# A sample-conditional adapter and linear layer on one core: half of the up projection in rounded parts, and x turned one sample ahead

## The reference

```python
h = relu(x @ W1[lang] + b1[lang])          # 512 -> 128: the up projection
y = x + h @ W2[lang] + b2[lang]            # 128 -> 512: the down projection
n = (y - mean(y)) * rsqrt(var(y) + 1e-5)   # over the 512 channels
x1 = x + n * gamma[lang] + beta[lang]
out = x1 + x1 @ W[cat] + b[cat]            # 512 -> 512
```

## Time and profile before

| what | value |
|---|---|
| median of 3 runs | 632.99 us (631.51 to 633.32) |
| the profiled execution | 632.66 us |
| its span in the trace | 630.8 us |
| instructions | 11158 |
| TensorE matmul (PE) busy | 620.4 us, 98% |
| VectorE (DVE) busy | 524.0 us, 83% |
| ScalarE (ACT) busy | 466.2 us, 74% |
| GpSimd (POOL) busy | 413.6 us, 66% |
| chain that ended last, share by engine | PE 95%, DVE 2%, DMA 1%, issue 1% |
| DMA | 166.00 MB, mean 263 GB/s |

### The profile page before, as it was taken

One profiled execution on the slowest core, in us unless ns is written; L12 is line 12 of the kernel. 1 busy time (PEld: TensorE's weight loads), 2 busy tenths in 40 slices (PEclk: granted clock), 3 DMA queues, 4 the chain that ended last, 5 costly groups with the idle time before them and its releaser, 6 DMA issues.

```text
span 630.8 us, 11158 instructions
## 1 busy us (share of the span) xinstructions
PE 620.4 (98%) x2773; PEld 474.5 (75%) x2773; DVE 524.0 (83%) x1155; ACT 466.2 (74%) x709; POOL 413.6 (66%) x326
## 2 busy tenths in 40 slices
PE   8799999999999999999999999999999999999997
PEld 7567877777877777877777877777877777877786
DVE  1879888889888889888889888889888889888873
ACT  3777777787777887777787777787777787777770
POOL 3947766666766666767666866766866766866630
PEclk9899999999999999999999999999999999999999
DMA  8848899888899888899898899988899798899422
GB/s 303 265 143 247 285 295 297 262 255 276 280 294 300 258 255 275 289 287 308 259 252 274 280 291 292 274 263 259 288 286 312 253 257 274 279 289 316 167 85 100
DMA packets 125562, 166.00 MB, mean 263 GB/s; under 512 B 10834, under 2 KB 72284, under 8 KB 121456
## 3 DMA queue, kind: packets, MB, share of 16 engines
q1 hardware_dynamic: 93540, 149.59, 72.6%
q10 hardware_dynamic: 32012, 16.30, 10.7%
HBM read 132.17 MB, written 33.55 MB: 263 GB/s over the span
## 4 chain that ended last, share of the span: by engine, by line
PE 95%; DVE 2%; DMA 1%; issue 1%; ACT 0%; ACTq 0%; SPq 0%; DVEq 0%
PE o_bank L730 18%; PE o_bank L728 18%; PE o_bank L729 18%; PE d_bank L756 17%; PE n_bank L744 9%; PE y_bank L728 2%; PE d_bank L728 2%; PE y_bank L730 2%; PE d_bank L730 2%; PE y_bank L729 2%; PE d_bank L729 2%; DMA x_tok<-in_x 1%; DVE y L587 0%; DVE xT L693 0%; PE n_bank L806 0%
## 5 line engine op out<-in xcount | busy, mean ns | idle before, releaser
L364 POOL TENSOR_TENSOR w_lo<-w_raw,w_hi 128x512 fp32r<-128x512 f32 x128 | 163.1, 1296 | 160.1 <-ACT w_hi L439 160.1
L728 PE MATMUL o_bank<-w_hi,x1T_hi 128*128 128x512 f32 x512 | 205.6, 402 | 0.0
L730 PE MATMUL o_bank<-w_hi,x1T_lo 128*128 128x512 f32 x512 | 200.5, 392 | 0.0
L729 PE MATMUL o_bank<-w_lo,x1T_hi 128*128 128x512 f32 x512 | 199.3, 389 | 0.0
L358 POOL TENSOR_TENSOR x_tok<-x_tok,b_bc 128x512 f32<-128x512 f32 x128 | 163.8, 1303 | 38.0 <-DMA b_bc<-in_L_cond_b 38.0
L429 ACT ACTIVATE norm<-y,neg_mean_rstd,rstd 128x512 f32<-128x512 f32 x127 | 153.4, 1284 | 0.1
L465 ACT ACTIVATE squares<-y,neg_mean 128x512 f32<-128x512 f32 x128 | 91.8, 718 | 76.6 <-DVE neg_mean L593 76.6
L632 DVE SCALAR_TENSOR_TENSOR n_bank<-n_bank,params,xT 128x512 f32<-128x512 f32 x128 | 93.3, 753 | 58.8 <-PE n_bank L744 58.8
L575 DVE STREAM_TRANSPOSE xT<-x_quad 128x512 f32<-128x512 f32 x120 | 125.2, 1087 | 3.2 <-issue 3.1
L756 PE MATMUL d_bank<-xT,w_raw 128*128 128x512 f32 x256 | 115.8, 594 | 3.2 <-DVE xT L693 1.7
L730 PEld LDWEIGHTS o_bank<-w_hi,x1T_lo 128*128 128x128 f32 x512 | 96.1, 188 | 21.2
(11 more groups left out here) (59 smaller groups left out, 524.9 us busy)
## 6 DMA issues: line engine op xcount, KB each, us to landing
w_raw<-in_L_cond_W SPq DMA_DIRECT2D x32, 1024.0 KB, 6.6
out<-out_half SPq DMA_DIRECT2D x63, 512.0 KB, 3.9
x_tok<-in_x SPq DMA_DIRECT2D x31, 1024.0 KB, 8.9
w_raw<-in_L_cond_W SPq DMA_DIRECT2D x64, 256.0 KB, 6.4
b_bc<-in_L_cond_b SPq DMA_DIRECT2D x64, 256.0 KB, 9.5
x_quad<-in_x SPq DMA_DIRECT2D x60, 256.0 KB, 3.9
x_quad<-in_x ACTq DMA_DIRECT2D x60, 256.0 KB, 3.9
x_tok<-in_x ACTq DMA_DIRECT2D x1, 512.0 KB, 3.3
```

Source lines behind the costliest of these rows:

```text
L364: pool.tensor_tensor(w_lo[q][:, c, :], w_raw[q][:, c, :], w_hi[q][:, c, :].bitcast(F32), ALU.subtract).then_inc(w_lo_done, 1)
L728: pe.matmul(acc, lhs_hi, rhs_hi, start=first, stop=False)
L729: pe.matmul(acc, lhs_hi, rhs_lo, start=False, stop=False)
L730: return pe.matmul(acc, lhs_lo, rhs_hi, start=False, stop=last)
```

## The change

- `up` from sample 2 on: chunks 2 and 3 stay float32 products and come first; chunks 0 and 1 are three products of rounded parts each. The parts of x (`xs_hi`, `xs_lo`) and of W1 (`w1_hi`, `w1_lo`) have one buffer each and are made in the step before: two copies on ScalarE behind `high_w2`, and three subtractions on GpSimd behind `low_w2`.
- VectorE turns sample s+1 in step s (`turn_next_x`). `xT` has three buffers and `x_quad` one, so the loads of x_quad of s+2 wait until s+1 is turned. With buffers of two and three, loops hold six steps: one round of six is written out, then comes the loop: four turns of it on TensorE, three on the other engines, which have the last round written out as well.
- SyncE loads W1 and W2 first in a step and x_quad after b; ScalarE issues its x_quad loads behind ReLU. GpSimd adds the second pair of b2 between the two pairs of w_lo.
- The start: TensorE turns x of sample 0 by tokens and not by chunks; x of sample 1 is turned in two halves around `down` of sample 0; the first normalisation is all on ScalarE, and its four chunks are turned together behind `down` of sample 1 with four banks. The loads of x_quad of sample 3, and behind them on ScalarE the parts of W1 and x of sample 2, wait for sample 2 to be turned.

```diff
+ROUND = 6
...
+        self.b, self.x = p % 2, p % 3
...
-        x_quad = [sb(f"x_quad{i}", [P, NB, NC * SQ]) for i in range(2)]
-        xT = [sb(f"xT{i}", [P, NC, T]) for i in range(2)]
+        x_quad = sb("x_quad", [P, NB, NC * SQ])
+        xT = [sb(f"xT{i}", [P, NC, T]) for i in range(3)]
...
                 if loads:
-                    sp.wait_ge(xT_done, k.count(NC, 0, 0))
-                    load_x_quads(k.sample(-1), q)
                     sp.wait_ge(y_done, k.count(NT, 0, 0))
+                    load_w1(lang, q)
                     load_w2(lang, q)
...
+                if quads:
+                    sp.wait_ge(xT_done, k.count(NC, 0, 2 * NC))
+                    load_x_quads(k.sample(-2))
...
+            def low_w1(k):
+                pool.wait_ge(w1_hi_done, k.count(1, 0, 0))
+                pool.tensor_tensor(w1_lo[:, :, :], w1_raw[1 - k.b][:, 0:NS, :], w1_hi[:, :, :].bitcast(F32),
+                                   ALU.subtract).then_inc(w1_lo_done, 1)
+            def low_xs(k):
+                pool.wait_ge(xs_hi_done, k.count(1, 0, 0))
+                for c in range(NS):
+                    pool.tensor_tensor(xs_lo[:, c, :], xT[(k.x + 1) % 3][:, c, :], xs_hi[:, c, :].bitcast(F32),
+                                       ALU.subtract).then_inc(xs_lo_done, 1)
...
                 if follow:
                     low_w2(q, k.count(1, -1, 1))
+                    if k.since(1):
+                        low_w1(k)
+                        low_xs(k)
...
+            def high_w1_of_next(k):
+                act.wait_ge(w1_in[1 - k.b], 16 * k.pairs(-1) + 16)
+                act.activation(w1_hi[:, :, :], w1_raw[1 - k.b][:, 0:NS, :], ACT.Copy).then_inc(w1_hi_done, 1)
+            def high_xs_of_next(k):
+                act.wait_ge(xT_done, k.count(NC, 0, NC + NS))
+                act.activation(xs_hi[:, :, :], xT[(k.x + 1) % 3][:, 0:NS, :], ACT.Copy).then_inc(xs_hi_done, 1)
...
-                if follow:
-                    load_next_x_quads(k)
                 if adapter:
                     relu(k)
+                if follow and not k.last(S - 2):
+                    load_next_x_quads(k)
                 high_x1(k, 0)
                 high_x1(k, 1)
                 if follow:
                     high_w2_of_next(k)
+                    high_w1_of_next(k)
+                    high_xs_of_next(k)
...
             def load_next_x_quads(k):
-                act.wait_ge(xT_done, k.count(NC, 0, 0))
-                load_x_quads(k.sample(-1), 1 - k.p)
+                act.wait_ge(xT_done, k.count(NC, 0, 2 * NC))
+                load_x_quads(k.sample(-2))
...
+            relu(k1)
+            for t in range(NT):
+                normalise(k1, t)
             high_w(k1, 0)
...
             high_w(k1, 2)
+            square(k1, 0)
+            square(k1, 1)
             high_x1(k1, 0)
             high_x1(k1, 1)
-            high_w2_of_next(k1)
-            square(k1, 0)
-            square(k1, 1)
+            square(k1, 2)
+            square(k1, 3)
             high_x1(k1, 2)
             high_x1(k1, 3)
-            square(k1, 2)
-            square(k1, 3)
             deviation(k1)
...
+            high_w2_of_next(k1)
+            load_next_x_quads(k1)
+            high_w1_of_next(k1)
+            high_xs_of_next(k1)
...
+            low_h(k1)
+            y_pair(k1, 0)
+            y_pair(k1, 1)
             x1(k1, 0)
             x1(k1, 1)
-            low_h(k1)
             low_x1(k1, 0)
             low_x1(k1, 1)
-            y_pair(k1, 0)
             x1(k1, 2)
             x1(k1, 3)
             low_x1(k1, 2)
             low_x1(k1, 3)
-            y_pair(k1, 1)
+            turn_next_x(k1, 0)
+            turn_next_x(k1, 1)
             variance(k1)
             inverse_deviation(k1)
+            turn_next_x(k1, 2)
+            turn_next_x(k1, 3)
...
-                for c in range(NC):
+                for c in range(parts, NC):
                     pe.wait_ge(xT_done, k.count(NC, 0, c + 1))
-                    ins = pe.matmul(d_bank[0][:, :], w1_raw[k.p][:, c, :], xT[k.p][:, c, :],
-                                    start=c == 0, stop=c == NC - 1)
+                    ins = pe.matmul(acc, w1_raw[k.b][:, c, :], xT[k.x][:, c, :], start=c == parts, stop=c == NC - 1 and not parts)
+                if parts:
+                    pe.wait_ge(w1_lo_done, k.count(1, 2, 1))
+                for c in range(parts):
+                    pe.wait_ge(xs_lo_done, k.count(NS, 2, c + 1))
+                    ins = split_product(acc, w1_hi[:, c, :], w1_lo[:, c, :], xs_hi[:, c, :], xs_lo[:, c, :],
+                                        False, c == parts - 1)
```

More of the change, by code:

```diff
@@ L138, in norm_bank @@
         def norm_bank(k, c):
-            return n_bank[c % 2]
+            return y_bank[c - 2] if c >= 2 and not k.since(2) else n_bank[c % 2]
         def by_chunk(k):
-            return k.since(2) and not (isinstance(k.h, int) and k.h == S // 2)
+            return k.since(2) and not k.last(S)
         def down_bank(t):
@@ L155, in adapter_then_conditional_linear @@
         first_b1_in = sem("first_b1_in")
-        xq_in = [sem(f"xq_in{i}") for i in range(2)]
+        xq_in = sem("xq_in")
         x_in = [sem(f"x_in{i}") for i in range(2)]
@@ L250, in store, with step @@
                              ).then_inc(stored[half], 16)
-            def step(h, p, loads=True, w_load=True, turn=True, linear=True):
-                k, q = Step(h, p), 1 - p
+            def step(h, p, quads=True, loads=True, w_load=True, turn=True, linear=True):
+                k = Step(h, p)
+                p, q = k.b, 1 - k.b
                 if loads:
@@ L309, in _ @@
             load_params(lang1, 1)
+            load_x_quads(2, range(NQ))
             step(0, 1, linear=False)
[L312 to L319, removed]
+            for p in range(2, 2 + ROUND):
+                step(0, p)
+            with sp.Fori(1, S // ROUND - 1) as h:
+                for p in range(2, 2 + ROUND):
+                    step(h, p)
+            for p in range(2, 2 + ROUND):
+                s = S - ROUND + p - 2
+                step(S // ROUND - 1, p, quads=s + 2 < S, loads=s + 1 < S)
+            step(S // ROUND, 2, quads=False, loads=False, w_load=False)
+            last = Step(S // ROUND, 3)
             store(last, 2, 0)
@@ L375, in step @@
                     if turn:
[L376 to L380, removed]
+                        plus_identity()
+                        for c in range(NC):
+                            low_w(c)
                 else:
@@ L398, in _ @@
             step(0, 1)
[L399 to L404, removed]
+            for p in range(2, 2 + ROUND):
+                step(0, p)
+            with pool.Fori(1, S // ROUND - 1) as h:
+                for p in range(2, 2 + ROUND):
+                    step(h, p)
+            for p in range(2, 2 + ROUND):
+                step(S // ROUND - 1, p, follow=S - ROUND + p - 1 < S)
+            step(S // ROUND, 2, adapter=False, follow=False)
         @block.scalar
@@ L586, in y_tile @@
                 dve.wait_ge(x_b2_done, k.count(NT, 0, t + 1))
-                dve.scalar_tensor_tensor(y[:, t, :], down_bank(t)[:, :], 1.0, x_tok[k.p][:, t, :],
+                if k.since(1) and not k.since(2):
+                    dve.wait_ge(norm_done, t + 1)
+                dve.scalar_tensor_tensor(y[:, t, :], down_bank(t)[:, :], 1.0, x_tok[k.b][:, t, :],
                                          ALU.mult, ALU.add, accum_out=y_sum[:, t:t + 1]
@@ L596, in y_pair @@
             def y_pair(k, i):
-                if i == 0 and k.since(1):
+                if i == 0 and k.since(2):
                     dve.wait_ge(norm_done, k.count(NT, 0, 0))
@@ L690, in _ @@
             y_pair(k0, 1)
-            for c in range(NC):
+            dve.wait_ge(xT_done, NC + 2)
+            for c in (2, 3):
                 dve.wait_ge(first_xT_turned, NC + c + 1)
@@ L710, in _ @@
             low_x1(k1, 3)
-            y_pair(k1, 1)
+            turn_next_x(k1, 0)
+            turn_next_x(k1, 1)
             variance(k1)
             inverse_deviation(k1)
-            with dve.Fori(1, S // 2) as h:
-                step(h, 0)
-                step(h, 1)
-            step(S // 2, 0, adapter=False)
+            turn_next_x(k1, 2)
+            turn_next_x(k1, 3)
+            for p in range(2, 2 + ROUND):
+                step(0, p)
+            with dve.Fori(1, S // ROUND - 1) as h:
+                for p in range(2, 2 + ROUND):
+                    step(h, p)
+            for p in range(2, 2 + ROUND):
+                step(S // ROUND - 1, p, follow=S - ROUND + p - 1 < S)
+            step(S // ROUND, 2, adapter=False, follow=False)
             for t in range(NT):
-                output(Step(S // 2, 1), t)
+                output(Step(S // ROUND, 3), t)
         @block.tensor
@@ L811, in _ @@
             pe.wait_ge(ident_done, 3)
-            for c in range(NC):
-                turn_first_x(k0, c)
+            turn_first_x()
```

193 lines of the change are left out of this document (107 added, 86 removed).

## The result

The changed kernel is slower: 636.05 us in the median of 18 runs (632.19 to 639.7) against 631.47 us (630.69 to 633.32) of the kernel before on the same chip, a ratio of 1.0065, 95% interval 1.0052 to 1.0077. The profiled execution took 635.48 us, with a span of 633.7, against 632.66 and 630.8. The forecast was 632.1, in a range of 627.5 to 637.5: the measured time lies inside the range, but the forecast had the change 0.6 us faster, with the gain of the steps just over the loss at the start, and it is slower, clear of noise.

What follows compares the result with a forecast made beforehand. TensorE, busy throughout the steady steps, was taken to bound the kernel. From 632.66 us, the steps gain 9.9, the start loses 7.6 and the clock 1.7, giving 632.1 us, in a range of 627.5 to 637.5.

Steps and rivals of the forecast that it cites:

- The gain in the step: Up projection on TensorE: six rounded matmuls replace two float32 chunks, saving 0.34 us a step, 9.9 us over steps 3 to 31.
- The start: Chain across engines before step 2: its transposes start at about 52.9 us for 45.3, a loss of 7.6 (5.4 to 10).
- The clock: TensorE at 1.2 GHz once behind the wait before step 2's transposes: a loss of 1.7 us (0 to 2.8).
- The failed step: DMA: x_quad of s+2 waits for the turn of s+1, is wanted 14 us later, and so is hidden.
- The sentence behind it: ScalarE's two issues behind ReLU: the copy of x1 can wait up to their 0.9 us, with more than 1 in hand.
- The fit of ScalarE and GpSimd: Added copies (1.47 us) and subtractions (3.25 us) fit into each step, leaving 0.8 us on ScalarE and 0.7 on GpSimd.
- The code rival: Longer loops are fetched again at jumps back, 2 us left over three times: 638 us, chance 0.25.
- The base: The kernel before: the sum starts from its profiled execution, 632.66 us, with the median of runs put 0.3 above that.

Runs made afterwards that it cites:

- two lines exchanged: The changed kernel with ScalarE's two x_quad loads at the start moved behind the rounding of W1 and x: 629.95 us, ratio 0.9983 to the kernel before.
- early loads: The changed kernel with two x_quad buffers, loads at the step's head on SyncE and ahead of ReLU on ScalarE: 628.51 us, ratio 0.9934 to the kernel before.

## Why the prediction was wrong

In the profiled executions the change costs 2.8 us, where the forecast had it 0.6 faster. Of these 3.4 us the late loads are 2.3, the clock 0.8 and the steps 0.6 (9.9 forecast, 9.0 and the 0.3 of the rest measured), less 0.3 at the start. So the miss is mostly one wait that was put at nothing. Without it the change would have come out at +0.5, which is no difference that can be told from noise.

- **The gain in the step** was 0.34, with a beat of 18.57. Measured: 0.32 and 18.586. Right. The Trainium skill ("FP8 and Floating Point Precision", section "TensorE Precision Notes") would have had 0.43 by its four passes for float32. The rows don't speak against four passes, but against taking a rounded product for one of them: a float32 chunk took 0.858 us, a quarter of it is 0.215, and three rounded products take 1.39 / 2 = 0.695, 0.23 each, so the gain is 0.16 a chunk and not 0.215.
- **The start** was 7.6 and measured 7.3, with `high_w` waiting for the identity and the transposes at 52.6 for 52.9. The chain laid out by hand held link by link. What I did not do with it was to ask which link was an order and which a dependence: 4.7 us of it fell with two lines exchanged.
- **The clock** was 1.7 us with ends of 0 and 2.8; it was 2.5. The term was sized by 3.3 us at half pace, copied from the dip of before. Here the clock was at 0.50 for 13.6 us, from 44.3 to 57.9. The last 5.3 of them, from 52.6 on, count: 2.65 us of work. It also fell earlier than foreseen, behind the wait for the low part of x and not in the wait in front of the transposes.
- **The failed step is the one on DMA**: "The x_quad of s+2 now waits for the turn of s+1 (ended about 7.5 us into the step) and is wanted 14 us later: hidden." The 14 us were nearly right for an undisturbed step: SyncE's loads of step 7 are issued at 146.91 and VectorE's next turn begins at 160.35, 13.4 us later. What failed is the landing. I took that of before, 3.9 us, for loads that then stood first in the step. Now they stand behind W1, W2, W, b2, x_tok and b, 3 MB, in step 15 issued from 293.6 on. At the 277 GB/s of the earlier trace rows, 1.7 MB have moved when x_quad is issued at 299.9; the other 1.3 MB and x_quad's own 1 MB need some 8.3 us more by this estimate. The median landing was 10.2, and the longest, the 14.22 us ahead of the turn of step 15, is past the window. Nor did I see that with one buffer a late turn makes the next issue late: in step 15 it comes 5.8 us behind the up projection, for 2.0 in step 7, and leaves 11.7 us until the next turn at 311.60. All this ate 2.3 of 9.0 us in the profiled execution. The sentence behind it, that the copy of x1 can wait for ScalarE's two issues, failed too where they took 2.08 us for 0.9.
- **The fit of ScalarE and GpSimd** was stated as a slack of 0.8 and 0.7 us a step. The sums were right, since the beat is clean with early loads. But I used that slack only to pass the added work, and never asked what a late turn would do to VectorE. Without the parts, 42.8 us of VectorE's waits cost 0.1 us; with them, such waits cost 1 to 4.
- **The code rival** had 0.25. The loops of six bring 31 instruction packets for 10, yet in the trace none falls between 280 and 500 us, in which TensorE jumps back twice, at 379.6 and 491.4, and the other engines within 7 us of it. With two buffers, and the same loops, no step is over 18.60. The rule of the Trainium skill on taken branches ("Runtime: NRT & Kernel Launch", section "Instruction fetch mechanics"), as the prediction applied it, would have had a stall at each jump; no run shows one that TensorE feels. The rival's time, 638, would have been nearly right, for another cause.
- **The base.** The profiled execution of before, 632.66, was above its median, 631.47. By the profiled executions the change costs 2.8 us, by the medians 4.6. The terms below account for the 2.8. For the other 1.8 there are the base (1.2) and the median of after lying 0.6 above its profile.

The sum as it should stand: -9.0 for the steps, +7.3 and +2.5 at the start, +2.3 for late loads, and -0.3 in the rest: +2.8.

**What stays open.** Why x_quad lands after 10 us in one step and 14 in the next, with the same loads in the same order, isn't settled. The first step over 19 us was step 6, 10, 12, 16 or 19, in different profiled executions of kernels with the parts and the same order of loads. Which effect of the parts gives the late loads their price isn't shown either. And whether the two buffers alone, without the earlier issue, would do was not tried.

## What to carry to other kernels

A load that is moved needs two new numbers, and neither is the old one: when it may be issued, and how many bytes stand ahead of it then; compare its landing with the time until its reader comes, not with the length of a step. With one buffer a late reader also sends the next load late, so one long landing is not over with its own step. Lateness that cost nothing may cost something once the steps are shorter and fuller, so price both together. A DMA issue that waits for a buffer blocks all that stands behind it on its engine; put it behind work that is ready.

## What the runs showed of the hardware

Loads of 256 KB landed in a median of 3.9 or 4.4 us when they were issued ahead of a step's other loads, in 7.4 between them and in 10.2 behind them. With the loads behind, the issue itself was slow in some steps, long or not: SyncE's pair took 3.84 us at 72.22, in step 3, which kept its 18.57 us, 2.93 at 279.81 and 1.10 at 299.89; with two buffers and early loads no pair of it took over 1.12. The stretch at the 1.2 GHz level was not the same length each time: 3.4 us in the kernel before, from 27.9, and 13.6 in the changed kernel, from 44.3. Matmuls on zeros, for 2.4 us in TensorE's first wait of step 2 and for 5.5 in the second, were enough to have none.
